# Range reduction of the phases rewritten, and the second expert matmul moved out of the first one's loop

## The chip, the cores and the metric

The kernel runs as one program on the 8 cores of one Trainium2 chip. The metric is device microseconds (us) of the slowest core. Engines are named as in the profile: PE (TensorE), DVE (VectorE), ACT (ScalarE), POOL (GpSimd) and SP (SyncE), the last two mostly issuing DMAs here.

## The reference, cut to what matters

```python
xn = layernorm(x)                                  # x: 4 x 4096 x 1024
k_real = xn @ Wk;  v = xn @ Wv                     # 16 heads of 64
k = exp(1j * 10 * k_real);  r = exp(1j * t * freqs)
out_pos   = real(cumsum(v * r) * conj(r)) / sqrt(t + 1)
out_assoc = real(cumsum(v * conj(roll(k, 1))) * k) / sqrt(t + 1)
attn = (g0 * out_pos + g1 * out_assoc) @ Wo
# experts: top 1 of 8 by the router's logits
for e in range(8):
    y = gelu(xn @ w1[e] + b1[e]) @ w2[e] + b2[e]   # 1024 -> 4096 -> 1024
    ffn += where(expert_idx == e, prob, 0) * y
out = x + attn + ffn
```

Every expert is computed for every token and masked afterwards.

## The kernel before, in words

Each core owns 2048 tokens (half of one batch row). The work has three stages.

Stage 1 (up to about 680 us of the span): layer norm of 2 x 16 tiles of 128 tokens, their transposes, the router, and the normalized activations written in bf16 to DRAM (`xnscr`).

Stage 2 (about 680 to 5737 us): experts and attention together. The loop over `gi` has 32 rounds, 8 experts times 4 chunks of 512 tokens. A round has the first matmul (f1, tile `f_h`): 8 blocks `cob`, each of 4 column tiles of 8 matmuls, 128x512, whose result goes through one of two PSUM buffers (`hps`) and a Gelu on ACT into `hsb`. PE may start column tile n only when the Gelu of tile n-2 is done. The second matmul (f2, tile `f_y`) has two halves `hh` of the 1024 outputs; a half is 8 pieces `kcg` of 16 matmuls, summed over in four PSUM buffers (`yps`), which DVE then scales and adds into `accf` (the evacuation). The second half may start only when DVE has evacuated the first (`tok_v_yev`), since it writes the same buffers.

In the kernel before, the pieces of f2's first half stand between the blocks of f1: `emit_f2_kcg(e, c, gi, 0, cob - 3)` follows block `cob` for `cob` 3 to 7, and pieces 5 to 7 follow the last block. The second half stands alone.

Every instruction stream is in program order. The attention is cut into 81 units, and `au_tick` deals them out over 320 places: after each of the 8 blocks (places 1 to 8), after f2's first half (9) and after its second (10). So there is a unit at every fourth place or so. Of the units 64 are channel tiles (`au_chtile`, 8 chunks x 8 tiles, 32 of them "fh", which only carry the running sums, and 32 "own", which also make output). By the formula in `au_tick` the places 1 to 7 and 10 get 49 of the 64 channel tiles (places 1 to 3 and 10 get 25, places 4 to 7 get 24), place 8 gets 7 and place 9 gets 8. A channel tile has on PE 16 matmuls (`a_kv`), on ACT a first part of five activations, on DVE the range reduction (line 667 on), on ACT a second part of six (sines and cosines), and on DVE four products and scans. ACT waits inside its queue for the range reduction (`tok_v_rr`), so Gelus that are queued behind a channel tile wait with it.

The range reduction brings an angle into [-pi, pi]: ACT writes angle/2pi plus a large constant (`MAGIC`), which rounds to an integer; DVE takes the constant off, multiplies by -2pi, adds the angle and clips.

Weights come as f32. POOL casts them in pieces (`emit_cast_pieces`) into bf16 copies in DRAM (`w1c`, `w2c`); each piece first waits for what PE had been given up to there (`T.tok`). SP loads `w1ring` (two slots of 1 MB, one per block of f1; a slot is free when the block two before is done), and POOL loads `f_w` from `w2c` (ten slots of 512 KB, one per piece of f2). Where an expert's casts are not yet given out when it starts, `force_casts_until` puts all the rest there, ahead of that round's `f_w` loads in POOL's queue. Before, a piece is given out after blocks 0, 3 and 6 of each round, 12 per expert against the 24 that one needs; the layer norm stage gives out 60 ahead.

Stage 3: the residual is added and the output written (about 100 us).

Of the kernel before, what the change touches and what calls it, by code (L numbers as in the profile page):

```python
# [7 lines left out]
F32 = mybir.dt.float32  # L8
BF16 = mybir.dt.bfloat16
AF = mybir.ActivationFunctionType  # L10
ALU = mybir.AluOpType
AX = mybir.AxisListType

P = 128
MAGIC = 12582912.0
TWO_PI = 6.2831854820251465
INV_2PI = 0.15915493667125702
PI_LO = 3.1415925025939941
# [105 lines left out]
def build_program(cfg: Cfg, phases=5):  # L124
    nc = bass.Bass("TRN2", target_bir_lowering=False)
    KT, DM, NCO, DFF, NE = cfg.KT, cfg.DM, cfg.NCO, cfg.DFF, cfg.NE
    NLT, TOWN, ACH, NACH, ATT = cfg.NLT, cfg.TOWN, cfg.ACH, cfg.NACH, cfg.ATT
    FCH, NTT, NFCH = cfg.FCH, cfg.NTT, cfg.NFCH
    W1CO, NW1C, NCOB, RING = cfg.W1CO, cfg.NW1C, cfg.NCOB, cfg.RING
# [3 lines left out]
    MMW = min(512, DM)  # L133
    NH = DM // MMW
    KCG = min(4, NCO)
# [41 lines left out]
    se_em = sbt("se_em", [NE, TOWN], BF16)  # L177
    carries = sbt("carries", [P, KT * 4], F32)
    bndc = sbt("bndc", [P, KT * 2], F32)
    consts = sbt("consts", [P, 4], F32)  # L180
    fcol = sbt("fcol_s", [P, KT], F32)
    f2col = sbt("f2col_s", [P, KT], F32)
    gposc = sbt("gpos_s", [P, KT], F32)
# [26 lines left out]
    with es:  # L210
# [106 lines left out]
        @block.vector  # L317
        def _(v):
            v = AE_V(v)
            v.memset(consts[:, 0:1], MAGIC)  # L320
            v.memset(consts[:, 1:2], PI_HALF)
            v.memset(consts[:, 2:3], 0.0)
            v.memset(consts[:, 3:4], 1e-5)
            v.memset(carries[:], 0.0)
            v.memset(bndc[:], 0.0)
            wvv.need(v, tok_setup_y)
            V.inc(v.tensor_scalar_mul(f2col[:], fcol[:], INV_2PI))
# [198 lines left out]
        with contextlib.ExitStack() as ph:  # L526
# [11 lines left out]
            sinph = psb("a_sph", [P, ACH + 1])  # L538
            pbuf = psb("a_p", [P, ACH])
            vsb = psb("a_vs", [P, 2 * ACH], BF16)  # L540
            cbuf = psb("a_cb", [P, ACH])
            tmpA = psb("a_tA", [P, ACH])
            tmpB = psb("a_tB", [P, ACH])
# [11 lines left out]
            kvp = [ph.enter_context(nc.psum_tensor("a_kv%d" % k_, [P, ACH], F32))  # L555
                   for k_ in range(2)]

            zcol_ap = lambda n: bass.AP(consts, 2, [[4, P], [0, n]])

            chunks = ([("fh", c) for c in range(NACH)] if phases >= 2 else []) + \  # L560
                     ([("own", c) for c in range(NACH)] if phases >= 3 else [])
# [41 lines left out]
            def au_chtile(ci, j):  # L603
# [42 lines left out]
                @block.scalar  # L646
                def _(s, ci=ci, j=j, gj=gj):
                    s = AE_S(s)
                    ws.need(s, tok_t_kv[(ci, j)])
                    ws.need(s, tok_y_trep[ci])  # L650
                    if gj >= 1:
                        pci, pjj = (gj - 1) // KT, (gj - 1) % KT
                        ws.need(s, tok_v_rr[(pci, pjj)])
                    if gj >= 2:
                        pci, pjj = (gj - 2) // KT, (gj - 2) % KT
                        ws.need(s, tok_v_p4[(pci, pjj)])
                    s.activation(vsb[:, (gj % 2) * ACH:(gj % 2 + 1) * ACH],
                                 kvp[1][:, 0:ACH], AF.Identity, scale=1.0)
                    s.activation(bphi[:], kvp[0][:, 0:ACH], AF.Identity, scale=10.0)
                    s.activation(bnphi[:], kvp[0][:, 0:ACH], AF.Identity,  # L660
                                 bias=consts[:, 0:1], scale=10.0 * INV_2PI)
                    s.activation(bthe[:], t_rep[:], AF.Identity, scale=fcol[:, j:j + 1])
                    s.activation(bnthe[:], t_rep[:], AF.Identity,
                                 bias=consts[:, 0:1], scale=f2col[:, j:j + 1])
                    tok_s_A[(ci, j)] = S.tok

                @block.vector
                def _(v, ci=ci, j=j, gj=gj):
                    v = AE_V(v)
                    wvv.need(v, tok_s_A[(ci, j)])  # L670
                    v.tensor_scalar(tmpA[:], bnphi[:], -MAGIC, -TWO_PI,
                                    ALU.add, ALU.mult)
                    v.tensor_tensor(bphi[:], bphi[:], tmpA[:], ALU.add)
                    v.tensor_scalar(bphi[:], bphi[:], PI_LO, -PI_LO, ALU.min, ALU.max)
                    v.tensor_scalar(tmpA[:], bnthe[:], -MAGIC, -TWO_PI,
                                    ALU.add, ALU.mult)
                    v.tensor_tensor(bthe[:], bthe[:], tmpA[:], ALU.add)
                    v.tensor_scalar(bthe[:], bthe[:], PI_LO, -PI_LO, ALU.min, ALU.max)
                    tok_v_rr[(ci, j)] = V.tok

                @block.scalar
# [137 lines left out]
            def emit_attn_units(upto):  # L819
                while au_idx[0] < min(upto, len(attn_units)):  # L820
                    attn_units[au_idx[0]]()
                    au_idx[0] += 1
# [30 lines left out]
                        tok_g_w2p[up] = D["gp%d" % slot].inc(  # L853
                            g.dma_start(dst, src))  # L854

            def emit_f2_kcg(e, c, gi, hh, kcg):
                up = (gi * NH + hh) * NKCG + kcg
                uh = gi * NH + hh
                slot = up % W2SLOTS

                @block.tensor
                def _(t, e=e, c=c, hh=hh, gi=gi, up=up, uh=uh, kcg=kcg,
                      slot=slot):
                    wt.need(t, tok_g_w2p[up])
                    wt.need(t, tok_s_h[(e, c, kcg * KCG + KCG - 1)])
                    if kcg == 0 and uh >= 1:
                        for tt in range(NTT):
                            wt.need(t, tok_v_yev[(uh - 1, tt)])
                    ins = None
                    for tt in range(NTT):  # L870
                        for k2 in range(KCG):
                            kc = kcg * KCG + k2
                            ins = t.matmul(  # L873
                                yps[tt][:, 0:MMW],
                                hsb[:, kc * FCH + tt * P:
                                    kc * FCH + (tt + 1) * P],
                                w2ring[:, slot * KCG * MMW + k2 * MMW:
                                       slot * KCG * MMW + (k2 + 1) * MMW],
                                start=(kcg == 0 and k2 == 0),
                                stop=(kcg == NKCG - 1 and k2 == KCG - 1))  # L880
                        if kcg == NKCG - 1:
                            tok_t_f2stop[(uh, tt)] = T.inc(ins)
                    tok_t_w2free[up] = T.inc(ins)
                    if hh == NH - 1:
                        tok_t_hsbfree[(gi, kcg)] = tok_t_w2free[up]

            def emit_f2_evacs(e, c, gi, hh):
                uh = gi * NH + hh
                for tt in range(NTT):
                    ttg = c * NTT + tt  # L890

                    @block.vector
                    def _(v, e=e, c=c, tt=tt, ttg=ttg, hh=hh, uh=uh):
                        v = AE_V(v)
                        wvv.need(v, tok_t_f2stop[(uh, tt)])
                        dst = accf[:, ttg * DM + hh * MMW:
                                   ttg * DM + (hh + 1) * MMW]
                        if e == 0:
                            v.tensor_scalar(
                                dst, yps[tt][:, 0:MMW],  # L900
                                se_tm[:, ttg * NE + e:ttg * NE + e + 1],
                                None, ALU.mult)
                        else:
                            v.scalar_tensor_tensor(
                                dst, yps[tt][:, 0:MMW],
                                se_tm[:, ttg * NE + e:ttg * NE + e + 1],
                                dst, ALU.mult, ALU.add)
                        tok_v_yev[(uh, tt)] = V.tok
                        if e == 0:
                            tok_v_acc[(0, c, tt)] = V.tok  # L910

            SLOTS_TOTAL = max(1, NCH * (NCOB + NH))
            au_slot = [0]

            def au_tick():
                au_slot[0] += 1
                emit_attn_units(au_slot[0] * len(attn_units) // SLOTS_TOTAL)

            for gi in range(NCH):
                e, c = gi // NFCH, gi % NFCH  # L920
# [21 lines left out]
                for cob in range(NCOB):  # L942
# [74 lines left out]
                        emit_f1_mms(ctb)  # L1017
                    tok_t_f1[(e, c, cob)] = (T, T.n)
                    au_tick()
                    if cob in (0, 3, 6):  # L1020
                        emit_cast_pieces(1)
                    if 0 <= cob - 3 < NKCG:
                        emit_f2_kcg(e, c, gi, 0, cob - 3)

                for g_ in range(min(NKCG, max(0, NCOB - 3)), NKCG):
                    emit_f2_kcg(e, c, gi, 0, g_)
                emit_f2_evacs(e, c, gi, 0)
                gpc[0] += NKCG
                if NH > 1:
                    emit_w2_pieces(e, 1, gpc[0])  # L1030
                    au_tick()
                    for g_ in range(NKCG):
                        emit_f2_kcg(e, c, gi, 1, g_)
                    emit_f2_evacs(e, c, gi, 1)
                    gpc[0] += NKCG
                au_tick()

            emit_attn_units(len(attn_units))
            finish_casts()
# [121 lines left out]
```

How the kernel before makes its waits and increments, by code:

```python
    def inc(self, instr):  # L52
        self.__init_seen()
        if id(instr) not in self._seen:
            self._seen.add(id(instr))
            self._keep = getattr(self, "_keep", [])
            self._keep.append(instr)
            instr.then_inc(self.sem, self.step)
            self.n += self.step
        return (self, self.n)
# [10 lines left out]
    def need(self, eng, tok):  # L71
        if tok is None:
            return
        if isinstance(tok[0], (tuple, list)):
            for t in tok:
                self.need(eng, t)
            return
        trk, val = tok
        if val is None or val <= 0:
            return
        key = id(trk)
        if self.wm.get(key, 0) < val:
            eng.wait_ge(trk.sem, val)
            self.wm[key] = val
# [433 lines left out]
                @blk  # L518
                def _(e):
                    e.wait_ge(sem_v, fence1[1])
# [528 lines left out]
                @blk  # L1049
                def _(e):
                    e.wait_ge(sem_v, fence3[1])
# [38 lines left out]
            @block.sync  # L1090
            def _(y):
                y.wait_ge(D["yout0"].sem, D["yout0"].n)
                y.wait_ge(D["yout1"].sem, D["yout1"].n)
            @block.gpsimd
            def _(g):
                g.wait_ge(D["yout0"].sem, D["yout0"].n)
                g.wait_ge(D["yout1"].sem, D["yout1"].n)
```

## Time and profile before

| what | value |
|---|---|
| time, median of 2 runs | 6333.38 us (6302.91 and 6363.85) |
| profiled execution, its own time | 5836.2 us |
| its span, core 7 (slowest) | 5834.7 us |
| spans of all cores | 5752.0 to 5834.7 us |
| PE busy | 4142.2 us, 71% |
| ACT busy | 1747.5 us, 30% |
| DVE busy | 1428.2 us, 24% |
| mean DMA | 139 GB/s |

The profile is of one execution. Busy shares are means over stages with different limits. Line 116 is the helper through which every DVE and ACT instruction goes, so those are told apart by tile. A row of a timeline gives start, duration, engine, line, operation, tiles, how many were merged, and in brackets the idle time before and what ended it.

### The profile page before, as it was taken

What the parts mean: (1) busy time and instruction counts of PE and PEld (TensorE: products, weight loads), DVE (VectorE), ACT (ScalarE), POOL (GpSimd) and SP (SyncE); (2) the same over time, 40 slices, a digit from 0 to 9 for tenths busy, and PEclk for the clock granted to TensorE, in tenths of its full rate; (3) what the DMA queues carried; (4) which work ended last, traced back from release to release, by engine and by line L of the source; (5) the groups of instructions that cost most, each with busy time, mean ns of one, the idle gap of its engine ahead of it and who ended that gap; (6) DMA issues with size and microseconds to landing.
All of it is one profiled execution on the core that took longest, in us unless ns stands there. A gap on an engine that the chain in (4) does not pass through costs nothing.

```text
span 5834.7 us, 52315 instructions; the slowest of 8 cores (5752.0 to 5834.7 us)
## 1 busy us (share of the span) xinstructions
PE 4142.2 (71%) x18224; PEld 1849.4 (32%) x18224; DVE 1428.2 (24%) x2651; ACT 1747.5 (30%) x2240; POOL 433.3 (7%) x727
## 2 busy tenths in 40 slices
PE   1022387787887778878897678767788788978882
PEld 0012233333333333333333233323333333333331
DVE  2133212222122222122214231113321223113221
ACT  1011123333333333333333232223322333233330
POOL 1000000000000000010000100000000100010000
PEclk9999998899998989988999889988899999989996
DMA  5856664444444555466555655474446745463333
GB/s 80 113 103 101 127 167 136 134 135 146 127 126 136 145 137 148 147 144 162 163 168 131 162 144 152 136 144 134 130 156 143 186 145 146 133 184 130 123 116 115
DMA packets 371632, 810.03 MB, mean 139 GB/s; under 512 B 71080, under 2 KB 246440, under 8 KB 337584
## 3 DMA queue, kind: packets, MB, share of 16 engines
q0 software_dynamic: 226624, 409.01, 31.7%
q1 hardware_dynamic: 144752, 397.69, 21.0%
q8 instruction: 151, 2.47, 0.2%
q14 instruction: 105, 0.86, 0.1%
HBM read 930.36 MB, written 157.29 MB: 186 GB/s over the span
## 4 chain that ended last, share of the span: by engine, by line
PE 56%; ACT 17%; DMA 10%; DVE 10%; issue 5%; DVEq 1%; ACTq 0%; SPq 0%; POOL 0%; POOLq 0%
PE f_y L873 27%; PE f_h L978 22%; ACT L116 8%; DMA w2c<-w 5%; ACT f_h L116 3%; DMA ln_x<-xfh 2%; PE a_kv L640 2%; PE a_kv L635 2%; DVE accf L116 2%; DVE ln_stg L116 1%; ACT a_bnt L116 1%; ACT a_bnp L116 1%; DMA o_x<-xown 1%; PE ln_tr L416 1%; DVE a_bth L116 1%
## 5 line engine op out<-in xcount | busy, mean ns | idle before, releaser
L978 PE MATMUL f_h<-f_xn,w1ring 128*128 128x512 bf16 x8192 | 1956.2, 396 | 744.2 <-ACT f_h L116 693.2
L873 PE MATMUL f_y<-f_w,f_h 128*128 128x512 bf16 x8192 | 1825.7, 383 | 264.2 <-DVE accf L116 148.5
L116 ACT ACT_TABLE_LOAD x432 | 554.3, 1283 | 3110.2 <-PE f_h L978 1757.1
L978 PEld LDWEIGHTS f_h<-f_xn,w1ring 128*128 128x128 bf16 x8192 | 810.5, 101 | 1860.6 <-issue 1024.1
L873 PEld LDWEIGHTS f_y<-f_w,f_h 128*128 128x128 bf16 x8192 | 805.0, 99 | 1257.9 <-issue 313.8
L116 ACT ACTIVATE f_h<-f_h,b_s 128x512 bf16<-128x512 f32 x1024 | 703.7, 687 | 758.6 <-PE f_h L978 731.7
L116 DVE TENSOR_SCALAR a_tA<-a_bnp 128x512 f32<-128x512 f32 x64 | 27.3, 427 | 1873.1 <-ACT a_bnt L116 1873.1
L116 DVE SCALAR_TENSOR_TENSOR accf<-f_y,se_tm,accf 128x512 bf16<-128x512 f32 x224 | 168.1, 751 | 1077.2 <-PE f_y L873 1056.5
L854 POOL DMA_DIRECT2D f_w<-w2c x512 | 274.0, 569 | 1750.6 <-PE f_y L873 1613.4
L416 PE MATMUL ln_tr<-ident_s,ln_xn 128*128 128x128 f32 x256 | 62.1, 423 | 392.6 <-DVE ln_xn L116 392.6
L116 DVE TENSOR_TENSOR_SCAN a_cb<-a_p,carries,consts 128x512 f32<-128x512 f32 x256 | 328.5, 1283 | 27.6 <-DVE a_p L116 1.4
L300 POOL DMA_DIRECT2D w2c<-w x128 | 91.4, 747 | 1905.9 <-PE f_h L978 1013.6
L416 PEld LDWEIGHTS ln_tr<-ident_s,ln_xn 128*128 128x128 f32 x256 | 50.2, 223 | 402.8 <-issue 402.8
L291 POOL DMA_DIRECT2D w1c<-w x64 | 55.1, 897 | 1457.8 <-PE f_h L978 898.6
L464 PE MATMUL ln_lg<-gw_s,ln_f 128*128 128x8 f32 x256 | 56.8, 360 | 107.3 <-DVE ln_f L116 107.3
L640 PE MATMUL a_kv<-a_xn,a_wv 128*128 128x512 bf16 x512 | 120.9, 379 | 0.0
L635 PE MATMUL a_kv<-a_xn,a_wk 128*128 128x512 bf16 x512 | 120.9, 379 | 0.0
L116 DVE COPY a_cph<-bndc 128x1 f32<-128x1 f32 x64 | 9.8, 154 | 387.1 <-ACT a_cth L116 387.1
L116 DVE CAST ln_stg<-ln_tr 128x128 bf16<-128x128 f32 x256 | 74.6, 291 | 98.7 <-PE ln_tr L416 74.5
L464 PEld LDWEIGHTS ln_lg<-gw_s,ln_f 128*128 128x128 f32 x256 | 55.8, 330 | 113.2 <-issue 113.2
L116 DVE BATCH_NORM_STATS2 ln_st<-ln_x 128x6 f32<-128x512 f32 x64 | 44.4, 694 | 161.0 <-DMA ln_x<-xfh 147.1
L782 PE MATMUL a_kv<-a_wo,a_z 128*128 128x512 bf16 x256 | 60.4, 378 | 24.7 <-DVE accf L116 24.7
(69 smaller groups left out, 1427.2 us busy)
## 6 DMA issues: line engine op xcount, KB each, us to landing
f_w<-w2c POOLq DMA_DIRECT2D x512, 512.0 KB, 7.3
w1ring<-w1c SPq DMA_DIRECT2D x256, 1024.0 KB, 5.8
w1c<-w POOLq DMA_DIRECT2D x64, 1024.0 KB, 17.9
w2c<-w POOLq DMA_DIRECT2D x128, 512.0 KB, 10.3
f_xn<-xnscr SPq DMA_DIRECT2D x32, 1024.0 KB, 8.8
a_wk<-wkc SPq DMA_DIRECT2D x64, 256.0 KB, 6.0
a_wv<-wvc SPq DMA_DIRECT2D x64, 256.0 KB, 6.3
ln_x<-xfh SPq DMA_DIRECT2D x16, 512.0 KB, 5.3
```

The lines of the kernel that those rows point to most:

```text
L116: ins = fn(*a, **k)
L291: sem.inc(g.dma_start(bass.AP(w1c, (_e * NCOB + cob) * P * KT * W1CO, [[KT * W1CO, P], [W1CO, KT], [1, W1CO]]), bass.AP(w1, _e * DM * DFF ...
L300: sem.inc(g.dma_start(bass.AP(w2c, ((_e * NH + hh) * NKCG + kcg) * P * KCG * MMW, [[KCG * MMW, P], [MMW, KCG], [1, MMW]]), bass.AP(w2, _e ...
L416: ins = t.transpose(trps[pr][:, kt * P:(kt + 1) * P], xnf[pr][:, kt * P:(kt + 1) * P], identsb[:])
L464: ins = t.matmul(lps[:, 0:NE], xnf32b[pr][:, kt * P:(kt + 1) * P], gwsb[:, kt * NE:(kt + 1) * NE], start=(kt == 0), stop=(kt == KT - 1))
L635: t.matmul(kvp[0][:, 0:ACH], wkb[:, kt * P:(kt + 1) * P], xna[:, kt * ACH:(kt + 1) * ACH], start=(kt == 0), stop=(kt == KT - 1))
L640: ins = t.matmul(kvp[1][:, 0:ACH], wvb[:, kt * P:(kt + 1) * P], xna[:, kt * ACH:(kt + 1) * ACH], start=(kt == 0), stop=(kt == KT - 1))
L782: t.matmul(kvp[hh][:, 0:MMW], zfm[:, jj * ACH + tt * P: jj * ACH + (tt + 1) * P], wob[:, jj * MMW:(jj + 1) * MMW], start=(jj == 0), stop=F ...
L854: g.dma_start(dst, src))
L873: ins = t.matmul(yps[tt][:, 0:MMW], hsb[:, kc * FCH + tt * P: kc * FCH + (tt + 1) * P], w2ring[:, slot * KCG * MMW + k2 * MMW: slot * KCG ...
L978: ins = t.matmul(hps[ctg % NHPS][:, 0:FCH], w1ring[:, slot * KT * W1CO + kt * W1CO + ct * P: slot * KT * W1CO + kt * W1CO + (ct + 1) * P], ...
```

## The change

It does four things.

1. The range reduction no longer uses the rounding constant. ACT adds 64.5 to angle/2pi and 64 times 2pi to the angle (two activations get a bias column that had none); DVE casts to int32 and back, finds by a comparison whether the cast rounded up, and subtracts 2pi times the integer. It is 7 DVE instructions per angle in place of 3, so 14 in place of 6 per channel tile.
2. f2's first half is no longer between the blocks of f1. A round is now 8 blocks of f1, then both halves of f2.
3. Cast pieces are given out at every fourth place of `au_tick`, 2.5 per round, in place of 3 per round.
4. A new tile `a_it`, and `consts` gets two more columns.

```diff
-            v.memset(consts[:, 0:1], MAGIC)
+            v.memset(consts[:, 0:1], 64.5)
+            v.memset(consts[:, 4:5], 64.0 * TWO_PI)
...
-                    s.activation(bphi[:], kvp[0][:, 0:ACH], AF.Identity, scale=10.0)
+                    s.activation(bphi[:], kvp[0][:, 0:ACH], AF.Identity,
+                                 bias=consts[:, 4:5], scale=10.0)
...
-                    s.activation(bthe[:], t_rep[:], AF.Identity, scale=fcol[:, j:j + 1])
+                    s.activation(bthe[:], t_rep[:], AF.Identity,
+                                 bias=consts[:, 4:5], scale=fcol[:, j:j + 1])
...
-                    v.tensor_scalar(tmpA[:], bnphi[:], -MAGIC, -TWO_PI,
-                                    ALU.add, ALU.mult)
-                    v.tensor_tensor(bphi[:], bphi[:], tmpA[:], ALU.add)
-                    v.tensor_scalar(bphi[:], bphi[:], PI_LO, -PI_LO, ALU.min, ALU.max)
...
+                    for vv_, th_ in ((bnphi, bphi), (bnthe, bthe)):
+                        v.tensor_copy(itmp[:], vv_[:])
+                        v.tensor_copy(tmpA[:], itmp[:])
+                        v.tensor_tensor(tmpB[:], vv_[:], tmpA[:], ALU.subtract)
+                        v.tensor_scalar(tmpB[:], tmpB[:], 0.0, TWO_PI,
+                                        ALU.is_lt, ALU.mult)
+                        v.scalar_tensor_tensor(th_[:], tmpA[:], -TWO_PI, th_[:],
+                                               ALU.mult, ALU.add)
+                        v.tensor_tensor(th_[:], th_[:], tmpB[:], ALU.add)
+                        v.tensor_scalar(th_[:], th_[:], PI_LO, -PI_LO,
+                                        ALU.min, ALU.max)
...
             def au_tick():
                 au_slot[0] += 1
                 emit_attn_units(au_slot[0] * len(attn_units) // SLOTS_TOTAL)
+                if au_slot[0] % 4 == 0:
+                    emit_cast_pieces(1)
...
                     au_tick()
-                    if cob in (0, 3, 6):
-                        emit_cast_pieces(1)
-                    if 0 <= cob - 3 < NKCG:
-                        emit_f2_kcg(e, c, gi, 0, cob - 3)
-
-                for g_ in range(min(NKCG, max(0, NCOB - 3)), NKCG):
-                    emit_f2_kcg(e, c, gi, 0, g_)
-                emit_f2_evacs(e, c, gi, 0)
...
+                for hh in range(NH):
...
+                        for kcg in range(NKCG):
...
```

PE's queue in the second round, from the block ahead of a channel tile at place 6. The kernel before:

```order
L978 MATMUL f_h<-f_xn,w1ring 128x512 x16
L621 UNCONDITIONAL_BRANCH
L635 MATMUL a_kv<-a_xn,a_wk 128x512 x8
L640 MATMUL a_kv<-a_xn,a_wv 128x512 x8
L861 UNCONDITIONAL_BRANCH
L873 MATMUL f_y<-f_w,f_h 128x512 x16
L962 UNCONDITIONAL_BRANCH
L978 MATMUL f_h<-f_xn,w1ring 128x512 x16
```

The changed kernel, the same place:

```order
L930 MATMUL f_h<-f_xn,w1ring 128x512 x16
L622 UNCONDITIONAL_BRANCH
L636 MATMUL a_kv<-a_xn,a_wk 128x512 x8
L641 MATMUL a_kv<-a_xn,a_wv 128x512 x8
L914 UNCONDITIONAL_BRANCH
L930 MATMUL f_h<-f_xn,w1ring 128x512 x16
```

The 16 matmuls of f2 that stood behind the channel tile's own are gone from there; the next pair of f1 tiles follows at once.

DVE's queue, the range reduction of a channel tile. The kernel before:

```order
L116 TENSOR_SCALAR a_tA<-a_bnp 128x512
L116 TENSOR_TENSOR a_bph<-a_bph,a_tA 128x512
L116 TENSOR_SCALAR a_bph<-a_bph 128x512
L116 TENSOR_SCALAR a_tA<-a_bnt 128x512
L116 TENSOR_TENSOR a_bth<-a_bth,a_tA 128x512
L116 TENSOR_SCALAR a_bth<-a_bth 128x512
```

The changed kernel, its first angle; the second has the same seven with `a_bnt` and `a_bth`:

```order
L115 CAST a_it<-a_bnp 128x512
L115 CAST a_tA<-a_it 128x512
L115 TENSOR_TENSOR a_tB<-a_bnp,a_tA 128x512
L115 TENSOR_SCALAR a_tB<-a_tB 128x512
L115 SCALAR_TENSOR_TENSOR a_bph<-a_tA,a_bph 128x512
L115 TENSOR_TENSOR a_bph<-a_bph,a_tB 128x512
L115 TENSOR_SCALAR a_bph<-a_bph 128x512
```

Six instructions have become fourteen, each waiting for the one before it, and ACT's sines wait for the last.

In POOL's queue the forced casts at the start of experts 3 to 7 are 10 pieces and then four times 12 in the kernel before, and 15 each time in the changed one (14 forced, and the one given out at the last place of the round before). They stand ahead of the eight `f_w` loads of that round in both.

## Rows read from the trace of the kernel before

**Rows 1.** Spans and granted clocks: a core's span, its clock, and a die's median.
```profile
core 1: 5821.2 us, clock 0.915
core 7: 5834.7 us, clock 0.912
die 0 (median of its cores): 5788.4 us, clock 0.916
die 1 (median of its cores): 5801.8 us, clock 0.916
```
**Rows 2.** Waits of PE, longest first: us in total, times, longest us.
```profile
PE f_h L978 <- ACT f_h L116: 693.2, 253, 14.0
PE f_y L873 <- DVE accf L116: 148.5, 24, 22.8
PE f_y L873 <- DMA f_w<-w2c: 115.7, 5, 30.7
PE f_h L978 <- DMA w1ring<-w1c: 48.4, 8, 27.8
```
**Rows 3.** Timeline of PE, a round with channel tiles at places 3 and 7.
```profile
1984.20 1.89 PE L635 MATMUL a_kv<-a_xn,a_wk 128*128 128x512 bf16 x8
1987.65 3.62 PE L978 MATMUL f_h<-f_xn,w1ring 128*128 128x512 bf16 x16
2004.87 5.06 PE L978 MATMUL f_h<-f_xn,w1ring 128*128 128x512 bf16 x16 [13.60 <-ACT f_h L116]
...
2042.94 1.89 PE L635 MATMUL a_kv<-a_xn,a_wk 128*128 128x512 bf16 x8
2046.39 3.62 PE L873 MATMUL f_y<-f_w,f_h 128*128 128x512 bf16 x16
2063.62 6.39 PE L978 MATMUL f_h<-f_xn,w1ring 128*128 128x512 bf16 x16 [10.16 <-ACT f_h L116]
```
**Rows 4.** Timeline of ACT and DVE beside the first of these stalls.
```profile
1993.20 0.43 DVE L116 TENSOR_SCALAR a_tA<-a_bnp 128x512 f32<-128x512 f32 x1 [20.46 <-ACT a_bnt L116]
1993.73 0.69 DVE L116 TENSOR_TENSOR a_bph<-a_bph,a_tA 128x512 f32<-128x512 f32 x1
1996.39 0.43 DVE L116 TENSOR_SCALAR a_bth<-a_bth 128x512 f32<-128x512 f32 x1
1996.95 1.28 ACT L116 ACT_TABLE_LOAD   x1 [3.92 <-DVE a_bth L116]
2002.74 1.28 ACT L116 ACT_TABLE_LOAD   x1
```
**Rows 5.** Groups by form: busy us, mean ns of one.
```profile
L116 DVE SCALAR_TENSOR_TENSOR accf<-a_kv,accf 128x512 bf16<-128x512 f32 x32 | 22.1, 691 | 202.1 <-PE a_kv L786 202.1
L116 ACT ACTIVATE a_bnp<-a_kv,consts 128x512 f32<-128x512 f32 x64 | 44.0, 688 | 6.5 <-ACT a_bph L116 0.8
L116 ACT ACTIVATE a_bph<-a_kv 128x512 f32<-128x512 f32 x64 | 38.2, 597 | 6.2 <-ACT a_vs L116 0.4
```
**Rows 6.** Timeline of PE: evacuation waits, with a channel tile at place 8 and without.
```profile
1149.37 30.30 PE L873 MATMUL f_y<-f_w,f_h 128*128 128x512 bf16 x128 [15.49 <-DVE accf L116]
...
2084.89 27.79 PE L873 MATMUL f_y<-f_w,f_h 128*128 128x512 bf16 x128 [1.07 <-DVE accf L116]
```
**Rows 7.** Timeline of PE at the start of expert 3.
```profile
2572.83 9.54 PE L978 MATMUL f_h<-f_xn,w1ring 128*128 128x512 bf16 x32 [4.27 <-DMA w1ring<-w1c]
...
2623.64 6.27 PE L873 MATMUL f_y<-f_w,f_h 128*128 128x512 bf16 x16 [14.35 <-DMA f_w<-w2c]
```
**Rows 8.** DMA in 2554 to 2618 us: queues, then issues, KB each, us to landing.
```profile
q0 software_dynamic: 5280, 5.24, 70.0%
q1 hardware_dynamic: 863, 4.72, 26.6%
...
w2c<-w POOLq DMA_DIRECT2D x10, 512.0 KB, 21.3
w1ring<-w1c SPq DMA_DIRECT2D x4, 1024.0 KB, 11.9
```
**Rows 9.** DMA issues of the whole span: KB each, median us to landing.
```profile
f_w<-w2c POOLq DMA_DIRECT2D x512, 512.0 KB, 7.3
w1ring<-w1c SPq DMA_DIRECT2D x256, 1024.0 KB, 5.8
```
**Rows 10.** Stretches: us, busy (x) of PE, PEld, DVE, ACT, POOL; PEclk, DMA share, GB/s.
```profile
1943.00:1973.00 30.00, 15.85 (x67) 6.53 (x65) 13.55 (x24) 15.95 (x21) 0.86 (x1) 0.77 0.06 17
2084.00:2112.00 28.00, 27.11 (x126) 12.33 (x127) 2.26 (x4) 0.00 (x0) 3.69 (x7) 1.00 0.39 132
```

More of the change, by code:

```diff
@@ L14 @@
 P = 128
-MAGIC = 12582912.0
 TWO_PI = 6.2831854820251465
@@ L179, in build_program @@
     bndc = sbt("bndc", [P, KT * 2], F32)
-    consts = sbt("consts", [P, 4], F32)
+    consts = sbt("consts", [P, 6], F32)
     fcol = sbt("fcol_s", [P, KT], F32)
@@ L540, in build_program @@
             vsb = psb("a_vs", [P, 2 * ACH], BF16)
+            itmp = psb("a_it", [P, ACH], mybir.dt.int32)
             cbuf = psb("a_cb", [P, ACH])
@@ L556, in build_program @@
                    for k_ in range(2)]
-            zcol_ap = lambda n: bass.AP(consts, 2, [[4, P], [0, n]])
+            zcol_ap = lambda n: bass.AP(consts, 2, [[6, P], [0, n]])
             chunks = ([("fh", c) for c in range(NACH)] if phases >= 2 else []) + \
@@ L670, in _ @@
                     wvv.need(v, tok_s_A[(ci, j)])
-                    v.tensor_scalar(tmpA[:], bnphi[:], -MAGIC, -TWO_PI,
-                                    ALU.add, ALU.mult)
-                    v.tensor_tensor(bphi[:], bphi[:], tmpA[:], ALU.add)
-                    v.tensor_scalar(bphi[:], bphi[:], PI_LO, -PI_LO, ALU.min, ALU.max)
[L675 to L678, printed above, removed]
+                    for vv_, th_ in ((bnphi, bphi), (bnthe, bthe)):
[9 more added lines that the diff above has]
+                                        ALU.min, ALU.max)
                     tok_v_rr[(ci, j)] = V.tok
@@ L854, in _ @@
                             g.dma_start(dst, src))
[L856 to L910, printed above, removed]
@@ L1019, in build_program @@
                     au_tick()
-                    if cob in (0, 3, 6):
-                        emit_cast_pieces(1)
-                    if 0 <= cob - 3 < NKCG:
-                        emit_f2_kcg(e, c, gi, 0, cob - 3)
-                for g_ in range(min(NKCG, max(0, NCOB - 3)), NKCG):
-                    emit_f2_kcg(e, c, gi, 0, g_)
-                emit_f2_evacs(e, c, gi, 0)
-                gpc[0] += NKCG
-                if NH > 1:
-                    emit_w2_pieces(e, 1, gpc[0])
-                    au_tick()
[L1032 to L1035, printed above, removed]
@@ L1036, in build_program, with _ @@
-                au_tick()
+                for hh in range(NH):
+                    up0 = gpc[0]
+                    uh = gi * NH + hh
+                    @block.tensor
+                    def _(t, e=e, c=c, hh=hh, gi=gi, up0=up0, uh=uh):
+                        for kcg in range(NKCG):
+                            up = up0 + kcg
+                            slot = up % W2SLOTS
+                            wt.need(t, tok_g_w2p[up])
+                            wt.need(t, tok_s_h[(e, c, kcg * KCG + KCG - 1)])
+                            if kcg == 0 and uh >= 1:
+                                for tt in range(NTT):
+                                    wt.need(t, tok_v_yev[(uh - 1, tt)])
+                            ins = None
+                            for tt in range(NTT):
+                                for k2 in range(KCG):
+                                    kc = kcg * KCG + k2
+                                    ins = t.matmul(
+                                        yps[tt][:, 0:MMW],
+                                        hsb[:, kc * FCH + tt * P:
+                                            kc * FCH + (tt + 1) * P],
+                                        w2ring[:, slot * KCG * MMW + k2 * MMW:
+                                               slot * KCG * MMW
+                                               + (k2 + 1) * MMW],
+                                        start=(kcg == 0 and k2 == 0),
+                                        stop=(kcg == NKCG - 1
+                                              and k2 == KCG - 1))
+                                if kcg == NKCG - 1:
+                                    tok_t_f2stop[(uh, tt)] = T.inc(ins)
+                            tok_t_w2free[up] = T.inc(ins)
+                            if hh == NH - 1:
+                                tok_t_hsbfree[(gi, kcg)] = tok_t_w2free[up]
+                    gpc[0] += NKCG
+                    if hh + 1 < NH:
+                        emit_w2_pieces(e, hh + 1, gpc[0])
+                    elif gi + 1 < NCH:
+                        pass
+                    for tt in range(NTT):
+                        ttg = c * NTT + tt
+                        @block.vector
+                        def _(v, e=e, c=c, tt=tt, ttg=ttg, hh=hh, uh=uh):
+                            v = AE_V(v)
+                            wvv.need(v, tok_t_f2stop[(uh, tt)])
+                            dst = accf[:, ttg * DM + hh * MMW:
+                                       ttg * DM + (hh + 1) * MMW]
+                            if e == 0:
+                                v.tensor_scalar(
+                                    dst, yps[tt][:, 0:MMW],
+                                    se_tm[:, ttg * NE + e:ttg * NE + e + 1],
+                                    None, ALU.mult)
+                            else:
+                                v.scalar_tensor_tensor(
+                                    dst, yps[tt][:, 0:MMW],
+                                    se_tm[:, ttg * NE + e:ttg * NE + e + 1],
+                                    dst, ALU.mult, ALU.add)
+                            tok_v_yev[(uh, tt)] = V.tok
+                            if e == 0:
+                                tok_v_acc[(0, c, tt)] = V.tok
+                    au_tick()
```

## The prediction

> **What bounds the kernel now.** I read first the clocks of the cores, to know that nothing disturbed the profiled execution: the two dies stand at 5788.4 and 5801.8 us with the same 0.916 [rows 1]. Then the waits of PE, because PE has by far the most work (71% busy) and is in the expert stage the engine that all others serve [rows 2]. They say where its idle time of stage 2 comes from: 693.2 us on Gelus, 148.5 us on evacuations by DVE, 115.7 us on `f_w` loads, and 48.4 us on `w1ring` (27.8 us of that is the first load of all). Third, the timeline around single waits, to see what a wait is made of. Of the 253 waits on Gelus about 204 last some 0.54 us and are part of every block of f1; these, 110 us, don't change. The other 49 hold the remaining 583 us, 11.9 us each, and there are just as many channel tiles at places that f1 follows. Two forms of them are to be seen [rows 3]: at place 3 PE has after `a_kv` two f1 tiles (3.6 us) and then stands for 13.60 us; at place 7 it has first 16 matmuls of f2 and then the two tiles, and stands for 10.16 us. The difference is the 3.45 us of the f2 piece. The chain is plain: Gelu of the tile two before waits in ACT's queue behind the channel tile's eleven activations, and these wait in the middle for DVE's range reduction [rows 4]. So DVE, 24% busy, is on the critical path 49 times with the whole of that reduction. The clock shows the second cost of a stall: in 1943 to 1973 us it is 0.77 on the mean against 1.00 in a stretch of f2 alone [rows 10], and the pair behind a stall takes 5.06 or 6.39 us in place of 3.6 [rows 3].
>
> **The range reduction.** Before, it takes from 1993.20 to 1996.82, 3.62 us: four TENSOR_SCALAR of 0.43 us, two TENSOR_TENSOR of 0.69 us, and five gaps of about 0.10 us [rows 4]. After, each angle has two casts, two TENSOR_TENSOR (0.69 each), two TENSOR_SCALAR (0.43 each) and one SCALAR_TENSOR_TENSOR with an immediate, whose nearest row is 0.691 us [rows 5]: 2.93 us plus two casts. The trace has no cast between two SBUF tiles of this size. Bounds are the fastest and the slowest row of the shape that it shows, 0.43 and 0.69 us. I take 0.43, the row of the other instructions with one tile as source. Two angles are then 2 x (2.93 + 0.86) = 7.6 us, with 13 gaps of 0.105 it is 8.9 to 9.0 us, that is 5.4 us more than now. ACT's two new biases cost what separates the activation with a bias from the one without, 688 - 597 = 91 ns each [rows 5], 0.2 us together. So 5.6 us per channel tile (6.7 us at the upper bound). At the 49 exposed places nothing hides it: ACT stands still meanwhile and both PSUM buffers of f1 are full. 49 x 5.6 = **+274 us** (330 at the upper bound). At place 9, half of f2, 27.8 us, stands behind `a_kv`; the chain of ACT and DVE ends after some 21 us even when longer, so nothing there.
>
> The Trainium skill (VectorE: DVE Perf Modes, "Mode 2×_2P — use both read ports for one tensor") says that an operation with one source and both sides in SBUF makes two results a cycle even in fp32, and that one with two sources can't. The rows of 0.43 and 0.69 us agree with that for TENSOR_SCALAR and TENSOR_TENSOR [rows 4]; whether it holds for a cast to and from int32 no row shows. By the rule the sum is the 274 us; if int32 fell out of it, 4 x 0.265 us more per tile, 52 us in all.
>
> **The lost cover.** At the 24 channel tiles of places 4 to 7 the f2 piece between `a_kv` and the next f1 pair is gone, so the stall has the longer form: 13.60 - 10.16 = 3.44 us each [rows 3]. 24 x 3.44 = **+83 us**. The f2 work isn't saved, it only stands later. The pair behind the shorter stall happened to run slower (6.39 against 5.06 us) [rows 3]; if that belongs to the form, 1.33 us per tile comes back, and the term is 51 us. I keep 83.
>
> **The evacuation of the first half.** With a channel tile at place 8, DVE is in its products and scans when f2's first half ends, and PE waits 15.49 us for an fh tile [rows 6], up to 22.8 us for an own tile [rows 2]. Before, four pieces of f2 (13.8 us) lie between; after, all eight (27.6 us). Each of the 7 waits gets 13.8 us shorter and 5.6 us longer: 7 x -8.2 = **-57 us**. The waits of 1.07 us elsewhere [rows 6] stay.
>
> **The casts at an expert's start.** POOL's forced casts end too late for f2's first piece: 14.35 us at expert 3 [rows 7], 115.7 us in five waits [rows 2], with about 14 us for `w1ring` beside them (4.27 us here [rows 7]) and some 2.5 us of slow clock behind each (6.27 us for 16 matmuls [rows 7]): 142 us. After, f2 first needs its weights after eight blocks in place of four. In the 64 us of expert 3's start ten pieces took 70% of the DMA time, 4.5 us each, and 4.72 MB on the other queue 27%, 3.6 us per MB [rows 8]. Fifteen pieces and the eight loads of a round are 67 + 29 = 96 us. PE needs eight blocks of 7.6 us and two channel tiles of about 3.5 + 19 + 1.5 us, 109 us. So the `f_w` wait goes. What is late next is `w1ring`: in this phase a load lands in 11.9 us [rows 8] while PE does a block in 7.6. With two slots that is (11.9 + 7.6) / 2 = 9.8 us per block, 2.2 us too long, for six blocks 13 us per expert. 142 - 5 x 13 = **-80 us**, between -130 (all hidden) and -20 (the longer burst reaches f2 after all).
>
> **w1ring in the other rounds.** Before, five of eight blocks gave a load 11 us, three gave 7.6. Now all give 7.6, and the median landing is 5.8 us [rows 9], so they fit, as the blocks 0 to 2 do now. But in every second round the cast at place 10 holds POOL until f2 ends, so that the eight `f_w` loads (4 MB) start together with f1. The third block's load then shares, with 11.9 us for 7.6 [rows 8]: about 4 us, in some ten rounds, some of it under a stall: **+30 us**, between 0 and +90.
>
> **The sum.** 274 + 83 - 57 - 80 + 30 = +250 us. The profiled execution was 5836.2 us, which would make 6086 us. The two timed runs lie at 6333.38 us, 497 us above it, and no row says why. The terms are waits of DVE, ACT and DMA in microseconds that don't hang on where that difference sits, so I carry them over as they are: 6333 + 250 = **6583 us**. Terms at their bounds: 274 + 51 - 57 - 130 + 0 = +138 (6471) and 330 + 83 - 50 - 20 + 90 = +433 (6766).
>
> **Rivals.** *The experts' starts give back nearly all.* The bursts vanish entirely (-142), no `w1ring` wait comes, the cover costs 51: 274 + 51 - 57 - 142 = +126 us, 6459 us, just within 2% (127 us), which is about what a measurement of this kernel tells from no change. For it speaks that the 96 us of DMA work are less than PE's 109; against it that the DMA engines are full there [rows 8] and the bursts grow to 15 pieces.
>
> *w1ring becomes the bound of f1.* If under ordinary traffic a load takes on the mean 9.6 us instead of 5.8, each of the five newly tight blocks waits 2 us: 32 x 5 x 2 = +320 us more, 6903 us. For it speaks that 1 MB per 7.6 us is 138 GB/s for this tile alone, near the whole kernel's mean; against it the three tight blocks of each round: of the 48.4 us [rows 2], 33 us fall in the first round and 14 us at the experts' starts, so that all others together wait some 1 to 2 us.
>
> *The added idle time buys clock, and the kernel is not slower.* The place is the 497 us between the timed runs and the profiled execution. In the profiled one the clock is 1.00 wherever PE works without a stall [rows 10]. If the timed runs are longer because all cores together were granted less, and the 350 us of new stalls, spread over the cores, lift that, then up to 497 us come back: 6333 - 497 + 250 = 6086 us, 4% faster. It turns at half: if 250 us come back, nothing is lost. Against it: PE's busy share falls only from 71% to some 68%, and stretches of 28 us of pure f2 remain as dense as they were, and longer. The Trainium skill (TensorE: Matmul & The Clock Gate, "Seeing it yourself") tells of a limiter that lowers the clock of a whole die once three of its cores run dense matmuls. The profiled execution, 1.00 in such stretches on a chip with eight busy cores, doesn't show it; by that rule the loss would stay in both kernels or, with less density, go.
>
> **Chances.** The forecast, with the terms near their values: 0.70. The experts' starts giving back all: 0.08. `w1ring` as bound, at half its price or more: 0.11. Clock given back: 0.11, split over faster (0.07), same (0.03) and a smaller loss (0.01). The range is 6440 to 6790: from the first rival to a little over the upper sum, leaving out the full `w1ring` case and the full clock case. Slower by over 2% (above 6460): 0.83. Within 2%: 0.10. Faster by over 2%: 0.07.
>
> **What would show it.** Right: the 49 long Gelu waits of one form, 19 us each, so `f_h` waits on ACT at about 693 + 357 = 1050 us; 14 DVE instructions of 0.43 and 0.69 us from the end of ACT's first part to its second, 9 us; the 15.5 us evacuation waits at 7 to 8; no `f_w` wait at experts 3 to 7, but `w1ring` waits of 2 to 4 us there. Wrong: casts of another length than 0.43 us; stalls behind channel tiles that stay at 14 us; `w1ring` waits spread over all rounds; a median in which the timed runs have come down to the profiled span.

## The result, and the profile after

The changed kernel is slower by 3.8%: ratio 1.038 to the kernel before, 95% interval 1.0341 to 1.0419. Its median over 11 runs is 6089.15 us, that of before over 10 runs 6018.07 us. The profiled executions are 6064.4 us of span against 5834.7, 230 us more. The ratio compares undisturbed runs only, which for the kernel before lie at 5833 to 5851 us but for one (5899 us), while executions of it at 6339 to 6403 us turned out to have the cores of one die at a mean clock of only 0.80 to 0.81, so the two runs around 6333 us were not typical of it.

The clocks of the slowest core and of the two dies:

```profile
core 6: 6064.4 us, clock 0.899
...
die 0 (median of its cores): 6034.9 us, clock 0.900
die 1 (median of its cores): 6037.7 us, clock 0.899
```

Both dies stand at the same clock, as in [rows 1]. The waits of PE answer to [rows 2]; columns are total us, times, longest us:

```profile
PE f_h L930 <- ACT f_h L115: 1046.2, 254, 19.8
...
PE f_h L930 <- DMA w1ring<-w1c: 95.8, 19, 28.8
PE f_y L991 <- DVE accf L115: 90.7, 24, 14.6
```

Against [rows 2]: the Gelu waits are 1046.2 in place of 693.2 us (+353.0), the evacuation waits 90.7 in place of 148.5 (-57.8), the `w1ring` waits 95.8 in place of 48.4 (+47.4), and the row of the `f_w` waits is gone (-115.7). The sum is +226.9 us; the spans differ by 229.7. Four rows of one view thus account for the change. PE's busy time went from 4142.2 to 4147.5 us with the same matmuls. Matmuls at a lower clock take longer and so count as more busy time; the longer stalls thus cost no more of slow clock than the shorter ones.

A stall of the new form, in the timeline of PE, which answers to [rows 3]:

```profile
2046.71 1.89 PE L636 MATMUL a_kv<-a_xn,a_wk 128*128 128x512 bf16 x8
...
2050.16 3.62 PE L930 MATMUL f_h<-f_xn,w1ring 128*128 128x512 bf16 x16
2073.23 9.58 PE L930 MATMUL f_h<-f_xn,w1ring 128*128 128x512 bf16 x32 [19.45 <-ACT f_h L115]
```

The 49 long waits now have one form: 46 of them last 19.1 to 19.8 us, and three 14.1 to 18.1 us. What they are made of stands in the timeline of DVE and ACT beside one of them, which answers to [rows 4]:

```profile
2116.89 0.43 DVE L115 CAST a_it<-a_bnp 128x512 int32<-128x512 f32 x1 [35.00 <-ACT a_bnt L115]
2117.42 0.43 DVE L115 CAST a_tA<-a_it 128x512 f32<-128x512 int32 x1
2117.95 0.69 DVE L115 TENSOR_TENSOR a_tB<-a_bnp,a_tA 128x512 f32<-128x512 f32 x1
...
2119.28 0.69 DVE L115 SCALAR_TENSOR_TENSOR a_bph<-a_tA,a_bph 128x512 f32<-128x512 f32 x1
...
2125.95 1.28 ACT L115 ACT_TABLE_LOAD   x1 [9.23 <-DVE a_bth L115]
```

ACT stands still for 9.23 us where it stood for 3.92 [rows 4]: 5.3 us more. Both casts take 0.43 us, the lower of the two bounds.

The evacuation waits at place 8, and one without a channel tile, answer to [rows 6]:

```profile
1161.67 30.40 PE L991 MATMUL f_y<-f_w,f_h 128*128 128x512 bf16 x128 [7.53 <-DVE accf L115]
1330.83 27.79 PE L991 MATMUL f_y<-f_w,f_h 128*128 128x512 bf16 x128 [1.07 <-DVE accf L115]
```

At the start of expert 3 (2674 to 2790 us) the DMA queues and issues answer to [rows 8], and the timeline of PE below them to [rows 7]:

```profile
q0 software_dynamic: 8506, 10.03, 62.0%
q1 hardware_dynamic: 2912, 9.96, 28.8%
...
w2c<-w POOLq DMA_DIRECT2D x15, 512.0 KB, 22.4
w1ring<-w1c SPq DMA_DIRECT2D x7, 1024.0 KB, 12.1
```

```profile
2703.17 5.19 PE L930 MATMUL f_h<-f_xn,w1ring 128*128 128x512 bf16 x16 [4.85 <-DMA w1ring<-w1c]
2755.83 3.61 PE L930 MATMUL f_h<-f_xn,w1ring 128*128 128x512 bf16 x16 [3.23 <-DMA w1ring<-w1c]
2777.82 5.30 PE L930 MATMUL f_h<-f_xn,w1ring 128*128 128x512 bf16 x16 [3.17 <-DMA w1ring<-w1c]
```

POOL issues fifteen casts in a row, a load of `w1ring` lands in 12.1 us (11.9 in the kernel before), PE waits for it three times, 11.3 us together, and never for `f_w`.

### The profile page after: what moved, and what is told of

The parts are those of the page before. It is cut to its first block, busy times and chain, and to the rows that moved or that the text cites. A ratio compares the mean times of both kernels' runs of the same rounds, so it can differ in the third digit from the quotient of the medians.

```text
span 6064.4 us, 53327 instructions; the slowest of 8 cores (6009.5 to 6064.4 us)
## 1 busy us (share of the span) xinstructions
PE 4147.5 (68%) x18224; PEld 1850.8 (31%) x18224; DVE 1716.0 (28%) x3164; ACT 1759.1 (29%) x2240; POOL 436.2 (7%) x727
## 4 chain that ended last, share of the span: by engine, by line
PE 55%; ACT 18%; DVE 14%; DMA 7%; issue 6%; DVEq 1%; ACTq 0%; SPq 0%
PE f_y L991 26%; PE f_h L930 22%; ACT L115 7%; DMA w1ring<-w1c 3%; ACT f_h L115 3%; DMA ln_x<-xfh 2%; DVE a_tB L115 2%; PE a_kv L641 2%; PE a_kv L636 2%; DVE a_bth L115 2%; DVE a_bph L115 2%; DVE accf L115 1%; ACT a_bnt L115 1%; DVE ln_stg L115 1%; ACT a_bnp L115 1%
## 5 line engine op out<-in xcount | busy, mean ns | idle before, releaser
L930 PE MATMUL f_h<-f_xn,w1ring 128*128 128x512 bf16 x8192 | 1955.6, 398 | 1142.2 <-ACT f_h L115 1046.2
L991 PE MATMUL f_y<-f_w,f_h 128*128 128x512 bf16 x8192 | 1795.2, 381 | 90.7 <-DVE accf L115 90.7
L115 DVE CAST a_it<-a_bnp 128x512 int32<-128x512 f32 x64 | 27.6, 432 | 1566.6 <-ACT a_bnt L115 1566.6
```

The costliest lines, as they stand in the source:

```text
L115: ins = fn(*a, **k)
L930: ins = t.matmul(hps[ctg % NHPS][:, 0:FCH], w1ring[:, slot * KT * W1CO + kt * W1CO + ct * P: slot * KT * W1CO + kt * W1CO + (ct + 1) * P], ...
L991: ins = t.matmul(yps[tt][:, 0:MMW], hsb[:, kc * FCH + tt * P: kc * FCH + (tt + 1) * P], w2ring[:, slot * KCG * MMW + k2 * MMW: slot * KCG ...
```

## The experiments

All ratios are to runs of the kernel before that were made beside each group of runs, on the same chip. The new range reduction and the moved f2 can be taken back one by one, and the first question is what each costs.

**e1: the old range reduction in the changed kernel.**

```diff
-                    for vv_, th_ in ((bnphi, bphi), (bnthe, bthe)):
...
+                    v.tensor_scalar(tmpA[:], bnphi[:], -MAGIC, -TWO_PI,
+                                    ALU.add, ALU.mult)
...
```

> The changed kernel with the range reduction of before (6 DVE instructions per channel tile) and all else as changed. Theory (the reduction costs 5.5 us at each of 49 exposed places, the moved f2 and its casts nearly cancel): 49 long Gelu waits of 13.6 us (666 us for them, 83 more than before), evacuation waits of about 2 us (fh) and 9 us (own) at place 8 (sum near 50 in place of 148.5 us), no f_w wait at the experts' starts (-116), w1ring waits near 96 (+47): +83 - 98 - 116 + 47 = -84 us against before, ratio 0.986. Rival A (the moved f2 is the costly part, the reduction is mostly hidden): ratio 1.02 to 1.03 against before.

There is no ratio with an interval for this run. The profiled execution took 5765.17 us, that of before 5836.2: 1.2% less. The waits of PE:

```profile
PE f_h L926 <- ACT f_h L116: 763.5, 252, 14.0
...
PE f_h L926 <- DMA w1ring<-w1c: 123.2, 29, 34.4
PE f_y L987 <- DVE accf L116: 50.4, 23, 9.0
```

The longest Gelu wait is back at 14.0 us, evacuation waits are 50.4 us in all, as worked out. `w1ring` waits are 27 us above what was expected. By this one execution, moving f2 is not the costly part; e5 below has the ratio.

**e2: only the new range reduction, in the kernel before.** The edit is the change's part 1.

> The kernel before with only the new range reduction. Theory: each of the 49 long Gelu waits grows by 5.5 us (+270) and each of the 7 evacuation waits at place 8 by the same (+38): +308 us, ratio 1.053, larger than that of the whole change. Rival A (mostly hidden, DVE is busy 24% only): under +100 us, ratio under 1.017.

Ratio 1.0535, interval 1.0512 to 1.0558.

```profile
PE f_h L985 <- ACT f_h L116: 965.5, 251, 19.8
...
PE f_y L880 <- DVE accf L116: 186.3, 23, 28.4
```

Gelu waits grow by 272.3 us and evacuation waits by 37.8 us against [rows 2], 310 in all, where 308 were expected. This part alone is slower than the whole change. DVE is idle for 72% of the span, and yet nothing of its added work is hidden.

**e5: only f2 moved.** Range reduction and cast places as before.

> The kernel before with only f2's first half moved behind f1; range reduction and cast places as before. Theory: like run e1, whose profiled execution was 72 us shorter than before's: ratio 0.985 to 0.99, no f_w waits at the experts' starts, w1ring waits of 110 to 125 us. Rival (the gain of e1 came from the cast places): 1.00 or more.

Ratio 0.9852, interval 0.9829 to 0.9876: the move by itself makes the kernel 1.5% faster. Its waits:

```profile
PE f_h L924 <- ACT f_h L116: 774.7, 248, 14.1
...
PE f_h L924 <- DMA w1ring<-w1c: 105.8, 18, 34.7
...
PE f_y L987 <- DVE accf L116: 51.4, 24, 9.0
```

Against [rows 2] that is +81.5 for the lost cover, -97.1 for evacuations, -115.7 for `f_w` and +57.4 for `w1ring`: -74 us, the spans differ by 65. And 1.0535 x 0.9852 = 1.038, the ratio of the whole change. The two parts simply combine, and within the intervals nothing is left for the cast places.

**e3: the cast places of before in the changed kernel.**

```diff
-                if au_slot[0] % 4 == 0:
-                    emit_cast_pieces(1)
...
+                    if cob in (0, 3, 6):
+                        emit_cast_pieces(1)
```

> The changed kernel with the cast pieces given out after blocks 0, 3 and 6 as before, so 12 forced pieces per expert start and no cast ahead of the next round's f_w loads. Theory: w1ring waits in the first three blocks of every second round go (some 20 to 30 us), those at the experts' starts shrink: 20 to 40 us faster than the changed kernel, ratio to before about 1.033. Rival B (w1ring is tight because every block of f1 has only 7.6 us): w1ring waits stay near 96 us and nothing moves, 1.038.

Ratio 1.042 (1.0378 to 1.0462), which doesn't differ clearly from 1.038. `w1ring` waits are 109.4 us in place of 95.8; in sum they did not fall, and the time is as rival B has it. Outside the first round and the five experts' starts with forced casts they went from 32.0 to 25.3 us, and at those starts from 31.1 to 45.7 us. So by these two executions the cast ahead of the `f_w` loads accounts for some 7 us, not for 20 to 30. e5 shows that the move of f2 brings the waits (48.4 us before, 105.8 with the move alone); that they come from f1's blocks following each other in 7.6 us fits this, but no run tests it by itself.

**e4: the new reduction at place 9 only.** `newrr = (au_slot[0] - 1) % 10 == 8` chooses, per channel tile, between both forms.

> The kernel before, with the new range reduction only at the 8 channel tiles of place 9, which 27.8 us of f2 follow. Theory (DVE work costs only where f1 follows within its reach): no change, within 0.2%, long Gelu waits as before. Rival C (more DVE work costs everywhere by its own length): 8 x 5.5 = 44 us, ratio 1.0075.

Ratio 1.0038 (1.0005 to 1.0071): half of what rival C asks, and more than the theory's 0.2%. The rows side with the theory in what the reduction could touch: Gelu waits 695.6 us against 693.2, evacuation waits 147.0 against 148.5. What grew are `f_w` waits (127.5 against 115.7) and `w1ring` waits (65.0 against 48.4), which differ by about as much between other kernels (104.9 and 59.4 us in e2). The time alone doesn't settle it; the waits speak for the theory.

**e6 to e8: the reduction out of ACT's way.** If the stall is the length of ACT's two parts plus the reduction in one piece, then cutting the channel tile in two attention units must shorten it, and the new reduction must become nearly free.

```diff
+            def au_chtile_b(ci, j):
...
                 @block.scalar
                 def _(s, ci=ci, j=j, gj=gj):
                     s = AE_S(s)
                     ws.need(s, tok_v_rr[(ci, j)])
...
                     attn_units.append(lambda ci=ci, j=j: au_chtile(ci, j))
+                    attn_units.append(lambda ci=ci, j=j: au_chtile_b(ci, j))
```

> The kernel before with each channel tile cut in two attention units: first a_kv, ACT's first part and DVE's reduction, then, two places or so later, ACT's sines and DVE's products. ACT no longer stands in its queue for the reduction. Theory (the long Gelu waits are ACT's parts plus the reduction in one piece): in place of 49 waits of 11.9 us two shorter ones per tile, 3.7 and 5.6 us without an f2 piece ahead and 0.3 and 2.1 us with one, some 300 us in all against 583, shorter evacuation waits (-80) and less slow clock behind stalls (-50): -350 to -400 us, ratio 0.935 to 0.95. Rival (more interruptions, each with its table load of 1.28 us on ACT and a low clock behind it, cost what is saved): 0.98 to 1.02.

> The changed kernel with the same cut of the channel tiles, the new range reduction kept. Theory: the reduction is now beside other work everywhere, so that its 8 more DVE instructions per tile cost nothing; Gelu waits of 3.7 and 5.6 us at the places 1 to 7 and 10, some 475 us against 935 in the changed kernel: ratio to before 0.95 to 0.965, equal to e8 within 0.5%. Rival (the reduction costs by its length wherever it stands): 4 to 5% above e8.

> As e7, with the range reduction of before: f2 and casts as changed, tiles cut in two. Theory: equal to e7 within 0.5%, and some 0.95 to 0.96 of before; slower than e6 by 1 to 2%, since without the f2 pieces between the blocks every Gelu wait has its long form. Rival: 4 to 5% below e7.

| run | f2 | reduction | ratio (interval) | Gelu waits us | `f_w` waits us | PE busy us |
|---|---|---|---|---|---|---|
| e6 | between | old | 0.9383 (0.9348 to 0.9417) | 341.4 | 169.9 | 4122.1 |
| e7 | moved | new | 0.9752 (0.9698 to 0.9805) | 491.2 | 137.3 | 4248.3 |
| e8 | moved | old | 0.9660 (0.9612 to 0.9708) | 489.0 | 123.6 | 4226.8 |

The reduction cost 5.35% when ACT waited for it in its queue. Between e7 and e8 it is 0.9% of the time of before, with intervals that overlap, and 2.2 us of Gelu waits. It was the waiting place, not the work, that cost. The 0.5% expected was missed if the ratios are taken as they are; of the 50 us between the two profiled spans 21 us are PE's busy time and 14 us `f_w` waits.

e6 met its range, though with other terms than expected: `f_w` waits grew from 115.7 to 169.9 us, presumably because PE now reaches the experts' starts sooner (not tested by itself). e7 and e8 came out above their ranges, by 0.01 and 0.006, and e8 is 3.0% slower than e6 where 1 to 2% was expected. The traces show two things that the expectations left out. The `f_w` waits that the move of f2 had removed are back. And PE is busy for 4226.8 us in e8 against 4140.4 in e5, with the same matmuls: 86 us of slow clock. The timeline of e8 shows it, and then that of e6:

```profile
2221.26 8.75 PE L932 MATMUL f_h<-f_xn,w1ring 128*128 128x512 bf16 x32 [4.25 <-ACT f_h L116]
2230.55 3.61 PE L932 MATMUL f_h<-f_xn,w1ring 128*128 128x512 bf16 x16 [0.54 <-ACT f_h L116]
```

```profile
1608.36 3.61 PE L984 MATMUL f_h<-f_xn,w1ring 128*128 128x512 bf16 x16 [0.54 <-ACT f_h L116]
...
1620.81 3.61 PE L984 MATMUL f_h<-f_xn,w1ring 128*128 128x512 bf16 x16 [1.93 <-ACT f_h L116]
...
1685.76 8.43 PE L984 MATMUL f_h<-f_xn,w1ring 128*128 128x512 bf16 x32 [5.38 <-ACT f_h L116]
```

32 matmuls take 7.07 us at full clock. Behind a stall of 4.25 us they take 8.75, behind 5.38 us 8.43, and behind one of 19.45 us 9.58 (above). Behind 1.93 us the next 16 take 3.61, with no loss at all. Summed up over PE's waits on ACT or DVE, the excess of the matmuls right behind a stall is 2.1 us on the mean behind 12 to 16 us (28 in before), 2.2 us behind more than 16 us (48 in the changed kernel), 1.8 us behind 3 to 5 us (49 in e8), and 0.1 us behind 1.5 to 3 us (24 in e6, nearly all of 1.93 us). So a stall of 3 us or more costs its length and, on the mean, some 2 us of slow clock, nearly whatever its length. Between 1.93 and 3 us the rows are mixed. Two of e8:

```profile
2469.42 7.07 PE L932 MATMUL f_h<-f_xn,w1ring 128*128 128x512 bf16 x32 [2.91 <-ACT f_h L116]
...
2514.61 8.75 PE L932 MATMUL f_h<-f_xn,w1ring 128*128 128x512 bf16 x32 [2.62 <-ACT f_h L116]
```

The longer of these two stalls lost nothing and the shorter one 1.7 us.

This is why one stall of 19 us has one charge, like one of 14, while the two stalls of 4 and 5 us that replace it in the cut form have two. It is also part of why the f2 pieces, which bring these down to 1.93 us or less, are worth more in the cut form than in the whole: moving f2 gains 1.5% with whole tiles (e5) and loses 3.0% with cut ones (e8 against e6; e8 has the changed cast places too, which e3 found to be worth nothing clear). Against e6, e8 has 147.6 us more of Gelu waits and 104.7 us more of busy PE, and 46.3 us less of `f_w` waits; e5 had only 81.5 us more of Gelu waits than before, no more busy PE, and 115.7 us less of `f_w` waits.

**e9 to e11: a version that beats both.** The casts forced at an expert's start are spread first.

```diff
-                    if cob in (0, 3, 6):
+                    if cob in (0, 2, 3, 5, 6):
                         emit_cast_pieces(1)
```

> The kernel before with five cast pieces per round (after blocks 0, 2, 3, 5 and 6) in place of three, so that nothing is left to force at an expert's start. Theory (the starts wait for casts that come in one piece, not for DMA rate in general): the f_w waits of 116 us go, and with them 2 us of slow clock each; w1ring waits grow by 0 to 30 us under the added casts: ratio 0.98 to 0.985. Rival (the casts' traffic costs wherever it is put): ratio 0.995 to 1.01, the waits turning up at w1ring.

Ratio 0.9886 (0.9766 to 1.0005), above the expected 0.98 to 0.985, with an interval that takes in these, part of the rival's range, and no change. So the time doesn't decide, and the waits do: `f_w` waits are down by 103.3 to 12.4 us, and `w1ring` waits are 77.9 us, 29.5 more, with two early waits of 34.8 and 18.1 us among them. The waits at the experts' starts are thus a matter of when casts are given out; somewhat over a quarter of what goes there comes back as `w1ring` waits.

> Run e6 (tiles cut in two, f2 pieces between the blocks) with five cast pieces per round. Theory: e6's f_w waits of 170 us go, ratio to before 0.938 - 0.029 + up to 0.005 for w1ring = 0.91 to 0.915. Rival: as for e9, 0.93 to 0.94.

Ratio 0.9167 (0.9130 to 0.9203), a little above the 0.91 to 0.915 expected and clear of the rival's, against 0.9383 for e6: the `f_w` waits fall from 169.9 to 15.8 us.

e11 is e10 with `emit_f2_kcg(e, c, gi, 0, cob - 2)` from block 2 on.

> Run e10 with f2's pieces from block 2 on (piece cob-2 behind block cob), so that place 3 is covered too. Theory: a stall of some 1.9 us after a covered place has no slow clock behind it, one of 4.0 or 5.4 us has 2 us; the 12 or so half tiles at place 3 get 3.5 us shorter and lose the 2 us: 30 to 60 us faster than e10, 0.90 to 0.905. Rival (the clock loss doesn't hang on the stall's length but on the number of stalls): 3.5 us each at best, under 40 us. If both are off, because a piece then waits for Gelus that ACT has late: no gain or a loss.

Ratio 0.9104 (0.9060 to 0.9148), median 5320.32 us. That is above the 0.90 to 0.905 expected, and the interval overlaps that of e10. The two profiled spans are 5359.0 and 5326.5 us, 33 us apart, at the lower end of the 30 to 60 us expected. Its waits:

```profile
PE f_h L984 <- ACT f_h L116: 316.4, 256, 5.4
PE f_y L879 <- DVE accf L116: 127.2, 22, 18.1
```

Gelu waits fell by 38.3 us against e10's 354.7. Evacuation waits rose by 31.7 (95.5 before), since one piece fewer of f2 stands between the last channel tile and the evacuation. The 33 us alone would also fit e11's rival. What tells them apart is core 7 of both runs: its Gelu waits over 3 us fell from 46 to 34, and those of 1.5 to 3 us rose from 26 to 32, with no loss behind any of them. PE's busy time, with the same matmuls, is 27.8 us less on the mean of cores 1 to 5 and 7 (4122.5 and 4094.7 us), for which both traces hold every matmul. So most of the gain is slow clock that is gone, as the theory had it. Seven evacuation waits of core 7 also came to 1.5 to 3 us, and four of these lost 1.6 to 1.7 us each, so the length alone doesn't decide there. This is the fastest version found: 9% faster than the kernel before and 12% faster than the changed one.

## Why the prediction was right or wrong

**The time, 6583 us (6440 to 6790), was wrong**; 6089.15 us lies outside. The step that failed is in "The sum": "I carry them over as they are: 6333 + 250". The added 250 us were near (the spans differ by 229.7), the base of 6333 us was not: the kernel before lies at 5833 to 5851 us. Two runs at 6303 and 6364 us beside a profiled execution of 5836.2 us should have cast doubt on the base and not only been noted ("no row says why"), and the profiled execution's own 5836 + 250 = 6086 us stood in the same paragraph, 3 us off the median. The range had no room for it, since that case was tied to the idea that *added idle time* buys the clock back. The runs show no such thing: the kernel before reaches its 5833 to 5851 us without any added idle time, and the changed kernel is 3.8% slower, not faster. That rival fell as a mechanism; that its number, 6086 us, is close to the measured one is luck.

**The ratio** was forecast as 6583 / 6333 = 1.039, with 0.83 on slower by over 2% (the cases as listed add up to 0.82). Measured 1.038. The match to the third digit is in part luck: two errors cancel, a sum that is 20 us too large and a base that is 500 us too large. On the base of 5836 us the same 250 us would have been 1.043. The direction and the mechanism were right. By its steps:

- *The range reduction, +274 us*: 5.6 us at 49 places. e2 gives +272.3 us for the Gelu waits, and single waits grow from 13.6 to 19.1 us. Casts take the lower bound, 0.43 us, as the Trainium skill (VectorE: DVE Perf Modes, "Mode 2×_2P — use both read ports for one tensor") would have it for an operation with a single source where source and result are in SBUF; this case's rows of 432 and 427 ns for f32 to int32 and back agree.
- *The lost cover, +83 us*: e5 gives +81.5. The alternative, that 1.33 us come back by the clock, fell: in the kernel before the slow clock behind the waits of 10 us and behind those of 14 us is 2.1 us on the mean for either form, and it is 2.2 us in the changed kernel.
- *The evacuation, -57 us*: measured -57.8, with 7.2 to 7.5 us and 14.2 to 14.6 us at the seven places. At e2 it is +37.8 as the same rule asks.
- *The casts at an expert's start, -80 us, and w1ring in the other rounds, +30 us*: together -50. `f_w` and `w1ring` together are -68.3 us. The `f_w` waits are gone. `w1ring` waits at the five starts are 31.1 us (13.9 before), where the term took 65; this is the term of the sum that was furthest off. In the other rounds they grew from 1.3 to 32.0 us. The size of the +30 is right, but by luck: 14.7 us of it are one single wait, and e3, which takes away the cast ahead of the `f_w` loads, still has 25.3 us there. e5 shows that they come with the move of f2.
- *w1ring becomes the bound of f1*: not so. Without the first load's 28.8 us its waits are 67 us in the changed kernel, in 32 rounds.
- *The experts' starts give back nearly all*: the `f_w` waits did vanish, but the other terms kept their size.

Left open is what decides whether a stall of 2 to 3 us is followed by slow clock, what sets the size of a single charge (mostly 1.3 to 2.9 us), and whether e4's 0.4% is anything but DMA waits.

## What to carry to other kernels

Look for the engine that waits inside its own queue for another one: here ACT for DVE's reduction, with Gelus behind it that PE needs. All work that this wait covers has the price of the critical path, however idle the engine that does it (DVE was busy 24% of the span). Cutting such a unit in two, so that other work stands between request and use, made that work nearly free. Shortening a stall from 4 us to 1.93 us gained more here than the difference in length, because the slow clock behind it went too. And when timed runs and profiled execution differ by 8%, forecast the ratio first, and give the range of the time room for either base.

## What the runs showed of the hardware

- The slow clock behind a stall costs about 2 us on the mean, nearly the same for stalls of 4 us (1.8 us, e8) and of 19 us (2.2 us, changed kernel). It was absent behind stalls of 1.93 us (0.1 us on the mean of 24 in e6), and behind stalls of 2.5 to 3 us it was there for some and absent for others (e8).
- Beside fifteen casts given out in one piece, a 1 MB load from SP landed in 12.1 us (median of 7); the median of the whole changed kernel is 5.6 us.
- On VectorE a cast of 128x512 between f32 and int32, in either direction, took 0.43 us, as long as a TENSOR_SCALAR of that size.
